# Induced phase: wide normalisations as scale and shift on ScalarE, biases and residual as products on TensorE, scattered rows turned back from the features

## The reference, cut to what matters

```python
def _layernorm(x, axis=-1, eps=1e-05):
    m = jnp.mean(x, axis=axis, keepdims=True)
    v = jnp.var(x, axis=axis, keepdims=True)
    return (x - m) / jnp.sqrt(v + eps)
...
def _mab(q, k, v, p):
    in_w, in_b, out_w, out_b, g1, b1, g2, b2, l1w, l1b, l2w, l2b = p
    x = q + _mha(_ln(q, g1, b1), _ln(k, g1, b1), _ln(v, g1, b1), in_w, in_b, out_w, out_b)
    h = _ln(x, g2, b2)
    ff = jax.nn.gelu(h @ l1w.T + l1b, approximate=False) @ l2w.T + l2b
    return x + ff
```

## Time and profile before

| what | value |
|---|---|
| median of 3 runs | 2460.18 us (2458.41 to 2463.89) |
| the profiled execution's own time | 2446.1 us |
| its span | 2444.3 us |
| mean granted clock of TensorE | 0.88 |
| induced phase in the span | about 1343 to 1948 us |
| busy in the span: PE, DVE, ACT, POOL | 83%, 54%, 46%, 32% |

### The profile page before, as it was taken

How to read it: one execution, slowest core, us unless ns; L and a number is a source line. 1 busy time by engine, 2 the same in 40 slices (tenths; PEclk the granted TensorE clock), 3 DMA queues, 4 the chain that set the end, 5 groups by cost and what they waited for, 6 DMA issues and landing times. The chain is left out here.

```text
span 2444.3 us, 43805 instructions
## 1 busy us (share of the span) xinstructions
PE 2019.2 (83%) x14601; PEld 1450.0 (59%) x14601; DVE 1323.6 (54%) x4329; ACT 1130.3 (46%) x2400; POOL 779.1 (32%) x975
## 2 busy tenths in 40 slices
PE   5799999999999999999995478867665179999944
PEld 4466666666666666666664356645443069999922
DVE  2365556656566555665562455776755223333358
ACT  2476656666666666665661134544432023333322
POOL 0012222222221222212222111235667625555543
PEclk7699999999999999999997566987776589999965
DMA  3641344213442144412400334522311477777622
GB/s 99 121 75 34 40 66 66 54 30 51 66 66 69 22 65 66 66 40 28 66 2 0 84 75 81 100 60 58 77 32 50 134 244 229 232 230 215 194 93 79
DMA packets 119393, 211.47 MB, mean 87 GB/s; under 512 B 23236, under 2 KB 52038, under 8 KB 118520
## 3 DMA queue, kind: packets, MB, share of 16 engines
q1 hardware_dynamic: 108024, 189.29, 34.9%
q0 software_dynamic: 10176, 17.09, 2.1%
q10 hardware_dynamic: 976, 2.30, 0.3%
HBM read 149.82 MB, written 66.82 MB: 89 GB/s over the span
## 5 line engine op out<-in xcount | busy, mean ns | idle before, releaser
L675 ACT ACTIVATE tower_prob<-tower_prob,tower_negmax 128x386 f32<-128x386 f32 (+1 forms) x768 | 390.5, 556 | 303.1 <-DVE tower_negmax L882 302.5
L882 DVE CUSTOM_DVE_ANT_0 tower_prob<-tower_sbank,tower_band 128x386 f32<-128x386 f32 (+1 forms) x768 | 346.4, 489 | 138.1 <-PE tower_sbank L449 132.9
L487 PEld LDWEIGHTS tower_tbank<-tower_ident,tower_prob 128*128 128x128 f32 x1920 | 227.6, 143 | 131.1 <-issue 81.0
L487 PE MATMUL tower_tbank<-tower_ident,tower_prob 128*128 128x128 f32 x1920 | 283.9, 278 | 23.2 <-DVE tower_probT L907 21.2
L731 ACT ACTIVATE tower_probT<-tower_tbank 128x384 f32<-128x384 f32 (+1 forms) x576 | 228.0, 431 | 126.3 <-PE tower_tbank L487 124.0
L2030 POOL DMA_INDIRECT scratch_yt<-experts_y,experts_rows x190 | 186.7, 983 | 202.4 <-DVE experts_y L2181 171.7
L426 PE MATMUL tower_dbank<-tower_oxT,tower_w 96*128 96x512 f32 x384 | 192.0, 625 | 12.1 <-ACT tower_oxT L720 12.0
L2089 PE MATMUL experts_ybank<-experts_w,experts_hid 128*128 128x128 f32 x1520 | 186.8, 277 | 0.0
L2118 ACT ACTIVATE experts_hid<-experts_hbank,experts_w 128x256 f32<-128x256 f32 x190 | 79.8, 471 | 224.4 <-PE experts_hbank L2077 224.4
L2077 PE MATMUL experts_hbank<-experts_zT,experts_w 128*128 128x256 f32 x760 | 182.1, 383 | 1.0 <-issue 1.0
L449 PE MATMUL tower_sbank<-tower_k_st,tower_q_st 49*128 49x386 f32 (+1 forms) x768 | 160.5, 412 | 26.3 <-POOL tower_k_st L631 13.6
(11 more groups left out here) (315 smaller groups left out, 3397.2 us busy)
## 6 DMA issues: line engine op xcount, KB each, us to landing
experts_w<-ew SPq DMA_DIRECT2D x95, 578.0 KB, 4.0
scratch_qk<-tower_qk SPq DMA_DIRECT2D x64, 384.0 KB, 4.7
tower_q_st<-scratch_qk SPq DMA_DIRECT2D x96, 192.0 KB, 8.2
tower_k_st<-scratch_qk SPq DMA_DIRECT2D x96, 192.0 KB, 11.2
experts_rows<-scratch_zs SPq DMA_DIRECT2D x95, 132.0 KB, 3.1
scratch_kq<-induce_kq SPq DMA_DIRECT2D x8, 1024.0 KB, 4.3
experts_res<-scratch_yt SPq DMA_DIRECT2D x8, 1024.0 KB, 5.6
induce_k_st<-scratch_kq SPq DMA_DIRECT2D x48, 128.0 KB, 4.3
```

The lines of the kernel that those rows point to most:

```text
L487: mm = pe.transpose(bank[:, jb * P:jb * P + P], prob[:, hg % PR, at + jb * P:at + jb * P + P], ident[:, :])
L675: act.activation(prob[:, hg % PR, 0:width(i)], prob[:, hg % PR, 0:width(i)], ACT.Exp, bias=negmax[:, hg % PR:hg % PR + 1], scale=-1.0).the ...
L882: scores.copied(dve.tensor_tensor_reduce(prob[:, hg % PR, 0:width(i)], bank[:, 0:width(i)], band[:, BAND_AT[i]:BAND_AT[i] + width(i)], sca ...
```

## The change

All edits are in `induce`.

- The wide normalisations (xs, x3, x2, yn, zn, x5) leave DVE. POOL now also makes a shift, −mean × rstd: two more small operations in each `root` of more than one tile and in each `twice`. ACT applies both with `centre`: four activations of the identity function with scale rstd and bias shift per item. The three normalisations of one tile only stay on DVE.
- The bias of the second block's output projection, added to x2 by POOL before, becomes a product in the bank of Y2: a row of ones against the bias row, 512 columns. In DOWN2's bank two such products are added ahead of the 16: the residual h against the identity matrix, and the second feed-forward bias. POOL's additions X2_BIAS and Y2_SUM go, and h2 becomes the bank plus y2. y2 has two buffers, and h one for each item.
- The rows of z are no longer made by POOL from zn. PE turns the scaled and shifted features zT back into rows (four transposes into a bank, key zR, at step GATE ahead of the gate products), and ACT copies that bank to all four slots of z in one operation (2048 numbers a partition, before 1536).

Cut to its core:

```diff
-        O2_OUT, O2_ROWS, O2_T, X2, X2_BIAS, Y2 = (74, 78), (76, 80), 82, 78, 80, 84
-        Y2_MOM, Y2_NORM, Y2_SUM, Y2_T = 85, 86, 87, 88
+        O2_OUT, O2_ROWS, O2_T, X2, Y2 = (74, 78), (76, 80), 82, 78, 84
+        Y2_MOM, Y2_NORM, Y2_T = 85, 86, 88
         UP2, DOWN2, Z_NORM, X5_NORM, Z_ROWS, Z_T = (98, 99), 101, 103, 105, 104, 106
-        GATE, GATE_1, GATE_2, Z_COPY, RANK, COEF, SLOT, STORE = 108, 109, 111, 112, 113, 114, 115, 118
+        GATE, GATE_1, GATE_2, Z_COPY, RANK, COEF, SLOT, STORE = 108, 109, 111, 108, 113, 114, 115, 118
...
-        NORMS = {A_NORM: FINAL, A_X3: HEAD, Y1_NORM: ATT1, R1_NORM: FF1, Y2_NORM: ATT2, Z_NORM: FF2}
+        NORMS = {Y1_NORM: ATT1, R1_NORM: FF1}
+        ACT_NORMS = {A_NORM: FINAL, A_X3: HEAD, Y2_NORM: ATT2, Z_NORM: FF2}
...
+            def bias_rows(bank, row, first_):
+                pe.matmul(bank[:, :].rearrange("p (t d) -> p t d", t=NT), onesr[:, :],
+                          erows[0:1, 1, row:row + 1, :].broadcast_to([1, NT, E]),
+                          start=first_, stop=False, skip_group_check=True)
...
-                    by_rows(("y2", m), o2T, wout[:, 1, :])
+                    bank = dense.claim(pe, ("y2", m))
+                    bias_rows(bank, BOUT, True)
+                    for t in range(NT):
+                        mm = pe.matmul(bank[:, t * E:t * E + E], o2T[:, t * P:t * P + P], wout[:, 1, :],
+                                       start=False, stop=True, skip_group_check=True)
+                    dense.filled(mm, ("y2", m))
...
+                    pe.matmul(bank[:, :], ident[:, :], h[m % NH][:, :, :].rearrange("p t d -> p (t d)"),
+                              start=True, stop=False, skip_group_check=True)
+                    bias_rows(bank, BL2, False)
...
+                    bank = dense.claim(pe, ("zR", m))
+                    for t in range(NT):
+                        mm = pe.transpose(bank[:, t * P:t * P + P], zT[:, 0, t * P:t * P + P], ident[:, :])
+                    dense.filled(mm, ("zR", m))
...
             def root(k, m, n=NT):
                 pool.wait_ge(moments, stat_order[k, m])
+                if n > 1:
+                    pool.tensor_scalar(shift[:, k, 1, 0:n], mv[:, k, 0:n, 0], -1.0, None, ALU.mult)
                 ch.mark(pool.tensor_scalar(rstd[:, k, 0, 0:n], mv[:, k, 0:n, 1], EPS, None, ALU.add))
                 ch.after()
-                pool.tensor_tensor(rstd[:, k, 0, 0:n], rstd[:, k, 0, 0:n], half[:, 0:n], ALU.pow).then_inc(roots, 1)
+                root_ = pool.tensor_tensor(rstd[:, k, 0, 0:n], rstd[:, k, 0, 0:n], half[:, 0:n], ALU.pow)
+                if n == 1:
+                    root_.then_inc(roots, 1)
+                else:
+                    ch.mark(root_)
+                    ch.after()
+                    pool.tensor_tensor(shift[:, k, 0, 0:n], shift[:, k, 1, 0:n], rstd[:, k, 0, 0:n], ALU.mult)                        .then_inc(roots, 1)
 
             def twice(k, m):
 
                 pool.wait_ge(moments, stat_order[k, m])
                 k = slot_of(k, m)
+                pool.tensor_scalar(shift[:, k, :, :], mv[:, k, None, :, 0].broadcast_to([P, 2, NT]), -1.0, None, ALU.mult)
                 pool.tensor_scalar(rstd[:, k, 0, :], mv[:, k, :, 1], EPS, None, ALU.add)
                 ch.mark(pool.tensor_scalar(rstd[:, k, 1, :], mv[:, k, :, 1], 1.0 + EPS, EPS * EPS, ALU.mult, ALU.add))
                 ch.after()
                 both = rstd[:, k, :, :].rearrange("p a t -> p (a t)")
-                pool.tensor_tensor(both, both, half[:, :], ALU.pow).then_inc(roots, 1)
+                ch.mark(pool.tensor_tensor(both, both, half[:, :], ALU.pow))
+                ch.after()
+                pool.tensor_tensor(shift[:, k, :, :], shift[:, k, :, :], rstd[:, k, :, :], ALU.mult).then_inc(roots, 1)
...
-                    if p == X2_BIAS:
-                        pool.wait_ge(x2_ready, m + 1)
-                        pool.tensor_tensor(x2[:, :, :], x2[:, :, :],
-                                           erows[:, 1, BOUT:BOUT + 1, :].broadcast_to([P, NT, E]), ALU.add)\
-                            .then_inc(x2b_ready, 1)
-                    if p == Y2_SUM:
-                        dense.wait_copied(pool, ("y2", m))
-                        if m:
-                            dense.wait_copied(pool, ("down2", m - 1))
-                        ch.mark(pool.tensor_tensor(y2b[:, :, :], y2[:, :, :], h[m % NH][:, :, :], ALU.add))
-                        ch.after()
-                        pool.tensor_tensor(y2b[:, :, :], y2b[:, :, :],
-                                           erows[:, 1, BL2:BL2 + 1, :].broadcast_to([P, NT, E]), ALU.add)\
-                            .then_inc(y2b_ready, 1)
...
-                        first = zm[:, :, 0, 0:E]
-                        ch.mark(pool.tensor_tensor(first, zn[:, :, :], grows[:, 0:1, :].broadcast_to([P, NT, E]),
-                                                   ALU.mult))
-                        ch.after()
-                        pool.tensor_tensor(first, first, grows[:, 1:2, :].broadcast_to([P, NT, E]), ALU.add)\
-                            .then_inc(z_ready, 1)
...
+            def centre(k, m, dst, src, sem, again=0):
+                act.wait_ge(roots, stat_order[k, m])
+                k = slot_of(k, m)
+                for t in range(NT):
+                    ins = affine(dst[:, t, :], src[:, t, :], rstd[:, k, again, t:t + 1], shift[:, k, again, t:t + 1])
+                ins.then_inc(sem, 1)
...
                 if p == Z_COPY:
-                    act.wait_ge(z_ready, m + 1)
-                    act.wait_ge(z_named, m + 1)
-                    zm = z[m % 2]
-                    act.activation(zm[:, :, 1:SLOTS, 0:E], zm[:, :, 0:1, 0:E].broadcast_to([P, NT, SLOTS - 1, E]),
-                                   ACT.Copy).then_inc(z_copied, 1)
+                    bank = dense.take(act, ("zR", m))
+                    if m >= 2:
+                        act.wait_ge(scattered[m % 2], 16 * NT * SLOTS * (m // 2))
+                        act.wait_ge(z_out, 16 * (m - 1))
+                    dense.copied(act.activation(
+                        z[m % 2][:, :, :, 0:E], bank[:, :].rearrange("p (t o d) -> p t o d", o=1, d=E)
+                        .broadcast_to([P, NT, SLOTS, E]), ACT.Copy), ("zR", m))
+                if p == A_NORM:
+                    centre(FINAL, m, xs[m], xs[m], centred)
+                if p == A_X3:
+                    if m:
+                        dense.take(act, ("u", m - 1))
+                    centre(HEAD, m, x3, h[m % NH], centred, 1)
+                if p == X2:
+                    if m:
+                        dense.wait_copied(act, ("y2", m - 1))
+                    centre(HEAD, m, x2, h[m % NH], x2_ready)
+                if p == Y2_NORM:
+                    if m:
+                        dense.take(act, ("t2T", m - 1))
+                    centre(ATT2, m, yn, y2[m % 2], centred)
+                if p == Z_NORM:
+                    if m:
+                        dense.take(act, ("zT", m - 1))
+                    centre(FF2, m, zn, h2, centred, 1)
+                if p == X5_NORM:
+                    if m:
+                        dense.take(act, ("x5T", m - 1))
+                        act.wait_ge(base_ready, m)
+                    centre(FF2, m, x5, h2, x5_ready)
...
-            def normalise(k, m, dst, src, sem, n=NT, again=0):
+            def normalise(k, m, dst, src, sem, n):
                 dve.wait_ge(moments, stat_order[k, m])
                 dve.wait_ge(roots, stat_order[k, m])
                 k = slot_of(k, m)
                 for t in range(n):
                     ins = dve.tensor_scalar(dst[:, t, :], src[:, t, :], mv[:, k, t, 0:1],
-                                            rstd[:, k, again, t:t + 1], ALU.subtract, ALU.mult)
+                                            rstd[:, k, 0, t:t + 1], ALU.subtract, ALU.mult)
...
-                if p == X2:
-                    normalise(HEAD, m, x2, h[m % NH], x2_ready)
```

76 lines of the change are left out of this document (25 added, 51 removed).

## The result

The changed kernel takes 2515.16 us (median of 4, 2511.07 to 2518.15) against 2460.8 before (median of 4): a ratio of 1.0219, 95% interval 1.0200 to 1.0239, or 54 us more. The forecast was 2497, 37 more, with a range to 2520: the direction was right, the loss half as large again as the sum.

The account below looks back on a forecast made before the run. No engine is full; a chain that changes hands sets the induced phase's period. At +4.0 us a period, seven periods give 27.1, plus front 6.6, entry 5.3, tail −2.0: +37.0 on the median 2460.18, forecast 2497, range 2460 to 2520.

Parts of the forecast that it names:

- front: First items, where nothing overlaps and TensorE waits out each normalisation: longer roots, xs and x3 cost +6.6 us (4.4 to 6.6).
- entry: Before the first h2: four added products, 3.8 us, and about 1.5 for ScalarE's normalisations, together +5.3 us.
- tail: Behind the last h2, GpSimd as the pace: two z additions go, the root grows, −2.0 us.
- (a): Statistics to yn: two lengthened roots, 1.1 us, and yn as four ScalarE operations, +0.4; together +1.5 us a period.
- low end: Statistics to yn: yn's stretch beside GpSimd's additions vanishes, so this piece costs only 0.8 us a period.
- (b): End of yn to the gates: ScalarE's fixed order makes x5 late, +1.0, and zR's transposes 0.65; +1.7 us a period.
- (d): Chosen to h2: three added 512-column products on TensorE, without a gap, +2.8 us a period; +5.6 at the lower clock.
- R3: Rival: gaps ahead of yn leave the added products at TensorE's lower clock, 2.8 us a period more; 2517, chance 0.14.
- (c): Gates to chosen: VectorE is the pace and only x2 leaves it, −1.97 us a period.
- The sign that I had named: TensorE's waits between the gates and chosen would go down by 2 to some 3.5 us.
- R1: Rival: VectorE, not TensorE, is the pace from yn to chosen; −1.2 us a period, 2453, chance 0.20.
- R2: Rival: ScalarE keeps up, x5 and the exponentials are never late and yn gains; 2482, chance 0.18.

Follow-up runs that it names:

- e2: Changed kernel with the three added 512-column products (output bias, residual h, second bias) left out, their terms missing from the result; 2490.96 us, ratio 1.0130.
- e7: Kernel before with the wide additions of the x2 bias and y2b done by VectorE instead of GpSimd; 2452.39 us, ratio 0.9974.
- e5: Changed kernel with nine idle 512-column products put on TensorE in its wait for yn; 2520.09 us, ratio 1.0255.
- e10: Changed kernel with yn, zn and x5 back on VectorE, without their shift operations; xs, x3, x2 stay on ScalarE; 2478.18 us, ratio 1.0087.
- e1: Changed kernel with all six wide normalisations back on VectorE and GpSimd's shift operations gone; added products and zR stay; 2467.98 us, ratio 1.0036.
- e8: Kernel before, unchanged, run and profiled again; 2455.18 us, ratio 0.9994.
- e9: Changed kernel with ScalarE's order moved: yn behind the exponentials of its step, zn one step later; 2513.45 us, ratio 1.0218.
- e6: Kernel with normalisations back on VectorE, added products and zR kept, but x2 alone moved to ScalarE with its shift on GpSimd; 2475.94 us, ratio 1.0065.

## Why the prediction was right or wrong, step by step

- **The front, the entry and the tail** came as worked out in their sums: +11.8 for +11.9, and −1.1 for −2.0. How the front and the entry share the 11.8 is not shown: e2, without the products of the entry, did not shorten it. The waits of PE for the first x3 and the second xs, 6.71 and 6.16 us in after, were 5.65 and 5.04:

```profile
1369.58 1.11 PE L1079 MATMUL induce_dbank<-induce_ident,induce_x 128*128 128x128 f32 x4 [6.71 <-ACT induce_x L1506]
1383.76 1.94 PE L1183 MATMUL induce_dbank<-induce_ident,x 128*96 128x128 f32 x8 [6.16 <-ACT x L1506]
```

- **(a)** The price was right where the step was undisturbed: 8.6 us from h2 to yn for 7.1, +1.5. For the first two periods the stretched yn of before vanished, as the low end had it, so the seven sum to +5.4, not +10.5. The Trainium skill's "ScalarE: Activation LUTs", section "Rules for kernel authors", which would keep such products on VectorE, points the right way here, and the traces agree: 1.65 us for yn on ScalarE, 1.17 on VectorE in e7.
- **(b) is the step that failed.** It was booked at 1.0 for ScalarE and 0.65 for zR and measured 3.8 a period on average. The order that makes x5 late was found, and its chain was sized well (6.5 forecast, 6.3 in e5). What was missed is what the lateness does to PE: e10 and e1 show PE running through without a gap and the full level back before the gates; in after it stops twice (0.91 and 0.20 us in the item shown) and is granted 0.50 to the gates, so that all its work there, some 15 us, is dear. zR stands with 1.11 in its row, not 0.65, for the same reason. The traces divide the 26.7 (e8 to after): 9.7 are longer waits of PE, 5.9 zR, and 11.1 PE's other work there, the same products, mostly at a lower clock. The periods bear it out. In the third, granted 0.80 before and 0.50 after, the piece grew by 5.0; in the fifth, granted 0.50 in both (before and after, columns as above), by 1.6, near the 1.7 forecast:

```profile
1782.00:1794.00 12.00, 11.32 (x56) 8.18 (x57) 8.59 (x15) 4.71 (x8) 10.47 (x11) 0.50 0.08 28
```

```profile
1832.00:1847.00 15.00, 13.13 (x64) 9.72 (x64) 2.88 (x5) 11.06 (x22) 11.83 (x14) 0.50 0.14 46
```

I had looked for the lower clock in the products of (d) (R3), which ran at the full level, 1.12 us as recorded, and not in the piece right behind the wait. The clock alone is not the cause, nor is ScalarE's order alone: with the clock full up to x5 (e5) PE waits for ScalarE, with ScalarE's order shortened (e9) ScalarE waits for PE; with yn, zn and x5 off ScalarE (e10) the piece falls to 77.0.
- **(c) failed too**, in its size and in the wait behind it: −14 became −4.2. The price, 1.97, was that of one stretched row. In five others x2 takes about 1.1, as in the e8 row below, and in the last of the seven it lies outside the piece; from start to start it gave 6.9 in all. The selection's own operations ga and gb, stretched in some periods of before, gave 5.1 more. Against both, DVE idles 7.8 us more in the piece. Of that 6.4 are two waits, 3.45 and 2.99 us, for which the profile names no releaser in the program; the row of after below is the first:

```profile
1757.01 1.11 DVE L1667 TENSOR_SCALAR induce_x<-induce_h,induce_mv,induce_rstd 128x128 f32<-128x128 f32 x4
```

```profile
1804.54 1.33 DVE L1742 TENSOR_REDUCE induce_peak<-induce_sbank 128x4 f32<-128x512 f32 x2 [3.45 <-remote]
```

Neither gc nor the wait for the scores explains it: gc costs the same before and after, and none of the 24.6 us lies in this piece. The sign that I had named failed with it: PE's waits between the gates and chosen did not fall from 5.46 to some 3.5, the rows above show 3.25 and 2.71. In e10, x2 on ScalarE too, the piece takes 56.7, 9.2 under e8; in e6 61.8, with idle time of the same kind as in after.
- **(d)** 18.7 forecast, 21.8 measured; e2, without the products, has 21.8 less in this piece. Right.
- **The rivals.** R1, DVE as the pace from yn to chosen, is refuted: with its work gone DVE is busy 3.9 of 17 us ahead of the gates, and the stretch is longer. R2, ScalarE keeping up, is refuted by e1 and e10. R3 had the right agent in the wrong place; over the whole period PE was granted 0.68, 0.73 before. The removed POOL additions did unstretch yn: 356 ns a tile in e7, 554 before. That agrees with the Trainium skill's "SBUF — State Buffer", section "SBUF: two separate sides", by which a VectorE and a GpSimd instruction can lock each other out of a shared pair of ports. e7 takes that gain without the rest, and it is 5 us, not enough to carry the change.
- **The total**: the errors are +14.8 in (b), +9.8 in (c), +3.1 in (d) and −5.1 in (a), with little elsewhere, 22.5 between the two profiles; between the medians, which no single execution bends, 17. That the range held is in part luck: it reached to 2520 for R3's price, the lower clock in the products of (d), and they ran at the full level.

Still open: the idle time that no releaser explains (e6, e10, and the two waits in after); it was not isolated, and in after it is 6.4 of the 9.8 that (c) lost. Open, too, is what the lower clock costs by itself between x5 and the gates.

## What to carry to other kernels

An engine with much spare time on the average is not free at the place where it is wanted: ScalarE stood idle three fifths of a period, but its fixed order put three normalisations between the root and the next products, and that cost 32 to 37 of the 54 us. A price read in one period is not yet that of seven: x2's 1.97 was the exception. Moving work off VectorE pays only if nothing else of that stretch waits for a later engine; look for the wait that will take its place. Where GpSimd's wide additions stretch VectorE's operations, VectorE may do them itself in a wait that it has anyway (0.66 and 0.69 us here, 1.27 each on GpSimd), which was the one small gain of this study.
